# Attention, mLSTM and expert layers on one core: an order per engine, maxima in bfloat16, a mask from 32-row products

## What is computed

```
x = x + attention(layernorm(x), W_qkv, W_out)        # 16 heads of width 16, causal
x = x + mlstm(layernorm(x), ctx, ctx, gates)         # 8 heads of width 32
x = x + experts(layernorm(x), router, up, down)      # 8 experts, 2 for each token

attn = softmax(q k^T / 4 + mask);  out = attn v      # mask: -1e10 where key > query
out = out.reshape(B, -1, S);  y = einsum("bds,nhd->bsd", out, W_out)
log_d = lf[t] - lf[s] + i[s], causal;  m = max_s(log_d);  d = exp(log_d - m)
h = (q k^T / sqrt(32) * d) v / (max(|sum_s|, exp(-m)) + 5e-5), then RMS-normed per head
```

## Time and profile before

| what | us |
|---|---|
| median of 3 runs | 974.06 (972.89 to 978.18) |
| the profiled execution | 972.35 |
| its span, first to last instruction | 970.6 |
| TensorE busy in the span | 880.4 (91%) |
| VectorE, ScalarE, GpSimd busy | 616.0, 490.8, 501.4 |
| mean clock granted to TensorE | 0.965 of full |

### The profile page before, as it was taken

One profiled execution on the slowest core, in us unless ns is written; L12 is line 12 of the kernel. 1 busy time (PEld: TensorE's weight loads), 2 busy tenths in 40 slices (PEclk: granted clock), 3 DMA queues, 4 the chain that ended last, 5 costly groups with the idle time before them and its releaser, 6 DMA issues.

```text
span 970.6 us, 31715 instructions
## 1 busy us (share of the span) xinstructions
PE 880.4 (91%) x11877; PEld 652.7 (67%) x11966; DVE 616.0 (63%) x1324; ACT 490.8 (51%) x839; POOL 501.4 (52%) x705
## 2 busy tenths in 40 slices
PE   4899999989997688999998998999999999999995
PEld 3566666766765445556665776878787878778783
DVE  4766776676767455679898677555555555555552
ACT  3566767767765556556664643333333333333331
POOL 2454756665665433357777677633444434444432
PEclk9899999999998988889998999999999999999998
DMA  8213343334244654355564433433232333233222
GB/s 273 66 24 88 84 112 113 80 89 140 78 88 138 131 174 146 101 160 177 186 193 134 122 73 91 99 67 51 47 51 46 53 49 51 46 51 51 46 35 23
DMA packets 133198, 92.97 MB, mean 96 GB/s; under 512 B 75712, under 2 KB 114112, under 8 KB 132928
## 3 DMA queue, kind: packets, MB, share of 16 engines
q1 hardware_dynamic: 119760, 73.10, 27.2%
q0 software_dynamic: 13296, 17.83, 11.2%
HBM read 54.65 MB, written 37.32 MB: 95 GB/s over the span
## 4 chain that ended last, share of the span: by engine, by line
PE 63%; DVE 11%; ACT 7%; DMA 6%; issue 4%; POOL 3%; SPq 3%; POOLq 0%; DVEq 0%; ACTq 0%
PE pair L963 19%; PE pair L977 10%; PE pair L979 7%; PE pair L665 4%; PE pair L687 3%; PE pair L701 3%; DMA o_scr<-On 3%; DMA STG<-wup_in 2%; PE pair L840 2%; PE pair L638 2%; ACT PT L1360 2%; PE pair L714 2%; PE pair L854 2%; DVE SD L1159 2%; PE pair L929 1%
## 5 line engine op out<-in xcount | busy, mean ns | idle before, releaser
L963 PE MATMUL pair<-XTs,WU 128*128 128x128 bf16 x3408 | 284.0, 219 | 7.7 <-DVE XTs L1303 4.0
L963 PEld LDWEIGHTS pair<-XTs,WU 128*128 x3408 | 237.7, 98 | 75.4 <-issue 12.2
L1637 POOL DMA_INDIRECT out_d<-XB x71 | 115.6, 1629 | 202.5 <-DVE XB L1325 168.8
L1503 ACT ACTIVATE Hf<-pair 128x512 f32<-128x512 f32 x142 | 84.9, 598 | 217.2 <-PE pair L963 217.0
L977 PE MATMUL pair<-WD,Hh 128*128 x479 | 181.1, 379 | 0.2
L1316 DVE CAST Hh<-Hf 128x512 bf16<-128x512 f32 x142 | 64.3, 453 | 164.5 <-ACT Hf L1503 160.2
L979 PE MATMUL pair<-WD,Hl 128*128 x568 | 154.8, 272 | 4.8
L1548 POOL TENSOR_SCALAR_AFFINE_SELECT PT<-PT 128x512 f32<-128x512 f32 (+1 forms) x96 | 74.7, 793 | 56.8 <-ACT PT L1354 52.0
L1318 DVE TENSOR_TENSOR Hl<-Hf,Hh 128x512 bf16<-128x512 f32 x142 | 99.7, 702 | 4.9
L1049 DVE TENSOR_REDUCE mxn<-pair 128x4 f32<-128x1024 f32 x64 | 75.2, 1216 | 27.4 <-PE pair L646 27.3
L1610 POOL DMA_INDIRECT xs_scr<-XB,WGf x64 | 68.6, 1071 | 28.2 <-issue 16.7
(11 more groups left out here) (245 smaller groups left out, 1756.5 us busy)
## 6 DMA issues: line engine op xcount, KB each, us to landing
XB<-xs_scr SPq DMA_DIRECT2D x71, 130.0 KB, 2.1
STG<-wup_in SPq DMA_DIRECT2D x32, 256.0 KB, 4.7
q_scr<-SPL SPq DMA_DIRECT2D x16, 512.0 KB, 4.2
STG<-wdn_in SPq DMA_DIRECT2D x32, 256.0 KB, 3.0
o_scr<-On SPq DMA_DIRECT2D x32, 128.0 KB, 4.1
Mm<-o_scr SPq DMA_DIRECT2D x16, 256.0 KB, 2.9
CnT<-ctxt_in SPq DMA_DIRECT2D x16, 256.0 KB, 4.5
CX<-ctx_in SPq DMA_DIRECT2D x16, 256.0 KB, 3.9
```

The source lines that it names most:

```text
L963: t = e.matmul(upb(j, k)[:, 128 * (fm % 4):128 * (fm % 4) + 128], WU[:, bass.ds(reg[j] * 4096 + off, 128)], XTs[:, r, hx, dk, :], start=n ...
L1503: e.activation(Hf[:, r, hs], upb(j, k), ACT.Gelu).then_inc(gel.sem, 1)
L1637: e.indirect_dma_start(out=out, out_offset=bass.IndirectOffsetOnAxis(ap=XS[:, i % NX, 256:257].bitcast(I32), axis=0), in_=Yf[:, i % NY, :] ...
```

## The change

**An order for each engine.** attn_steps takes an engine and reads a table ROUND, written like ORDER. On TensorE the cyclic order of a round stays, but for MG, which moves ahead of AX. ScalarE does the context split (A6c) and A6n earlier in the round. On GpSimd A6s stands ahead of the first weight split, the second split and A0s stand at the end of the round, A6c ahead of T2. The first gate chain (GT, Gs, Gp) is moved earlier on TensorE and ScalarE; on VectorE the step Gs now follows AX of the last item. The lines of ORDER are new as well.

```diff
+ROUND = {
+    "tensor": "T0:1:1 GT:15 S0:0 VX:0 T2:1 A4:2 MG:0 weights:0:2 AX:0 S1:-1:0 T0:0:0 PV:1 S1:-1:1 QK:-2",
...
+def attn_steps(engine):
+    parts = 0
+    for i in range(-4, B + 3):
+        for kind, lag, u in words(ROUND[engine]):
+            b = i - lag
...
-    "gpsimd": "sc:0 B4p:2 sc:0 R6:5 sc:0 split:0 split:0 B5s:2 rest:0:0 rest:0:1 rest:0:2 split:0",
+    "gpsimd": "R6:5 rest:0:0 sc:0 split:0 sc:0 split:0 split:0 B5s:2 B4p:1 sc:0 rest:0:1 rest:0:2",
...
+                    w.wait_ge(l_lm, 16)
                     for u in range(2):
                         pair_free(w, kind, *key, u)
                         for jj in range(2):
-                            e.matmul(out_[u][:, jj, :].rearrange("p (g c) -> p g c", c=wd)[:, :, wd - 128:wd], idb[:, :],
-                                     mkb[:, :].rearrange("p (a c) -> p a c", a=1).broadcast_to([128, n, 128]),
+                            rows = slice(64 * u + 32 * jj, 64 * u + 32 * jj + 32)
+                            e.matmul(out_[u][:, jj, :].rearrange("p (g c) -> p g c", c=wd)[:, :, wd - 128:wd], LM[rows, 0, :],
+                                     LM[rows, 1, :].rearrange("p (a c) -> p a c", a=1).broadcast_to([32, n, 128]),
                                      start=True, stop=False, skip_group_check=True)
...
                     else:
                         pair_left(w, 1)
+                        w.wait_ge(b_init, 1)
...
-            e.tensor_scalar(mv[:, :, 2], mv[:, :, 1], 1e-5, None, ALU.add).then_inc(var.sem, 1)
+            e.tensor_tensor(mv[:, :, 2], mv[:, :, 1], CF[:, C_EP:C_EP + 1].broadcast_to([128, 2]), ALU.add).then_inc(var.sem, 1)
...
                 elif kind == "S1":
+                    w.wait_ge(mpT.sem, mpT.at(b - 1))
+                    w.wait_ge(p_init.sem, p_init.at("Mp0"))
                     for u in range(2):
                         w.wait_ge(s1m.sem, s1m.at(b, P, u))
-                        e.tensor_reduce(mxn[:, 1, P, 2 * u:2 * u + 2, :], pair_of("S1", b, P, u)[:, :, :].rearrange("p j (r c) -> p j r c", r=2),
+                        e.tensor_reduce(Mph[:, 1, P, 2 * u:2 * u + 2, :], pair_of("S1", b, P, u)[:, :, :].rearrange("p j (r c) -> p j r c", r=2),
                                         AX.X, ALU.max, negate=True).then_inc(mx1.sem, 1)
...
-                elif kind == "Mp":
-                    w.wait_ge(mx1.sem, mx1.at(b, 1, 1))
-                    w.wait_ge(mx0.sem, mx0.at(b, 1))
-                    w.wait_ge(mpT.sem, mpT.at(b - 1))
-                    w.wait_ge(p_init.sem, p_init.at("Mp0"))
-                    e.tensor_copy(Mph[:, :, :, 0], mxv).then_inc(dvc.sem, dvc.up())
-                    w.wait_ge(dvc.sem, dvc.n)
-                    e.tensor_tensor(Mph[:, :, :, 1], mxv, Mph[:, :, :, 0], ALU.subtract).then_inc(mp_.sem, 1)
...
+            w.wait_ge(s0m.sem, s0m.at(B - 1, 1))
+            e.tensor_copy(mkb, CF[:, C_MASK:C_MASK + 128])
             link(e.memset(dsel[:, :, :], 0.0))
...
-                    e.tensor_scalar(XB[:, t0:t0 + 4, 259], KM, -1.0, 8.0, ALU.mult, ALU.add)
+                    e.tensor_tensor(XB[:, t0:t0 + 4, 259], CF[:, C_EK:C_EK + 1].broadcast_to([128, 4]), KM, ALU.subtract)
```

More of the change, by code:

```diff
@@ new lines, with words @@
+ROUND = {
[5 rows of a table added]
+}
+LIMITS = {"S1": (0, B - 1), "T0": (0, B - 1), "PV": (0, B - 2), "A0s": (0, B - 1), "A0n": (0, B - 1), "QK": (0, B - 1), "A6s": (0, B - 4),
+          "A6n": (0, B - 4), "S0": (0, B - 1), "VX": (0, B), "T2": (0, B - 1), "A6c": (0, B - 4), "A4": (0, B - 2), "AX": (-2, B), "MG": (0, B)}
+def words(line):
+    for word in line.split():
+        kind, lag, *u = word.split(":")
+        yield kind, int(lag), int(u[0]) if u else 0
+def attn_steps(engine):
[3 more added lines that the diff above has]
+            b = i - lag
+            if kind == "load":
+                if ok(b):
+                    yield kind, 2 * b, 0
+                    yield kind, 2 * b + 1, 0
+            elif kind == "split":
+                if ok(b):
+                    yield kind, parts, 0
+                    parts += 1
+            elif kind not in LIMITS:
+                if b == 0:
+                    yield kind, u, 0
+            elif LIMITS[kind][0] <= b <= LIMITS[kind][1]:
+                yield kind, b, u
@@ L169 @@
 ORDER = {
[5 rows of a table removed]
-}
-def entries(engine):
-    for word in ORDER[engine].split():
-        kind, lag, *u = word.split(":")
-        yield kind, int(lag), int(u[0]) if u else 0
[5 rows of a table added]
+}
 def mlstm_steps(engine):
@@ L190, in mlstm_steps @@
     for i in range(B):
-        for kind, lag, u in entries(engine):
+        for kind, lag, u in words(ORDER[engine]):
             b = i - lag
@@ L243, in of, with build @@
     return [s[1:] for s in steps if s[0] == kind]
-def build(nc, x, ctx_in, ctx_t, wqkv, wout, wg, bg, gain, wr, br, wup, wdn, cst, out):
+def build(nc, x, ctx_in, ctx_t, wqkv, wout, wg, bg, gain, wr, br, wup, wdn, cst, msk, out):
     xs = nc.dram_tensor("xs_scr", (XROWS, ROW), F32, kind="Internal").ap()
@@ L333, in build @@
         wtmp = OTs[:, 2, :]
[L334 to L335 removed]
+        Mph = Mp[:, :, :, :, 0:2]
         ca.close()
@@ L376, in build @@
         Hf = sb("Hf", [128, 2, 1024], F32)
-        steps = list(attn_steps())
+        pe_attn, dve_attn, act_attn, pool_attn, sp_attn = (list(attn_steps(n)) for n in ROUND)
         pe_steps, dve_steps, act_steps, pool_steps, sp_steps = (list(mlstm_steps(n)) for n in ORDER)
         dvc, poc = Chain(sem("dve_chain")), Chain(sem("pool_chain"))
+        l_lm = sem("l_lm")
         l_c, l_w, l_wo, l_wg, l_z = sem("l_c"), (sem("l_w0"), sem("l_w1")), sem("l_wo"), sem("l_wg"), sem("l_z")
@@ L403, in chunk @@
             return src[:, 512 * k:512 * k + 512], v[:, :, 0, :], v[:, :, 1, :], STG[:, c % 2, :].rearrange("p (a w) -> p a w", w=width)
-        lns = [s[:2] for s in steps + dve_steps if s[0] in ("A0s", "A6s", "B5s")]
+        lns = [s[:2] for s in dve_attn + dve_steps if s[0] in ("A0s", "A6s", "B5s")]
         LNK = {k: i % 4 for i, k in enumerate(lns)}
@@ L433, in build @@
         users = []
-        for kind, b, P in steps:
+        for kind, b, P in pe_attn:
             if kind in ("S1", "T0"):
@@ L1036, in vector_attn @@
         def vector_attn(e, w):
-            for kind, b, P in steps:
+            for kind, b, P in dve_attn:
                 if kind == "weights":
@@ L1338, in scalar_attn @@
         def scalar_attn(e, w):
-            for kind, b, P in steps:
+            for kind, b, P in act_attn:
                 if kind == "weights" and b < 2:
@@ L1549, in causal @@
                                 channel_multiplier=-1).then_inc(done.sem, 1)
-            for kind, b, P in steps:
+            for kind, b, P in pool_attn:
                 if kind == "weights" and b == 2:
@@ L1688, in sync_attn @@
                             onesb[:, :].rearrange("p (a c) -> p a c", a=1).broadcast_to([128, 2, 128])).then_inc(l_on, 16)
-            for kind, b, P in steps:
+            for kind, b, P in sp_attn:
                 if kind == "load":
```

119 lines of the change are left out of this document (39 added, 80 removed), and 12 rows, old and new, of tables (ORDER, ROUND).

## The result

The changed kernel takes **960.0 us** (median of four runs, 954.6 to 962.8) beside 973.5 of the kernel before in the same comparison: a ratio of 0.985, with an interval of 0.982 to 0.988. In a second comparison with more runs it was 0.981 (0.978 to 0.984). It is faster, inside the range, and by 13.5 us where 26.1 were forecast.

A forecast was written before the change was run, and what follows sets the result against it. TensorE's time was taken as the bound, plus where it stands still or is clocked down. 13.0 + 1.1 + 3.5 + 8.5 = 26.1 us off the profiled 972.35 gave 946.3, or a median of 948.0, range 941 to 955.

The forecast's parts named there:

- S1's masks: Attention round on TensorE: 32-row mask products run side by side, gaining 0.4 us a round for S1 part 1.
- rival 2: Attention masks don't run side by side, or writes of four banks hold each other up: 958 us, chance 0.06.
- Rival 3: Attention round is set by the DMAs, not TensorE, so 13 us are lost: 961 us, chance 0.07.
- S0's masks: Attention round on TensorE: shorter masks for S0, whose second half still waits for ScalarE's evacuation, gain 0.3 us a round.
- The tail: Attention round, from T2's end to T0's start: 4.60 us becomes 4.33, a gain of 0.27 us a round.
- The first item: Start of the attention, where no tail runs beside the masks: three masks give 0.4 + 0.4 + 0.3 = 1.1 us.
- The end of the attention: Last full round: A6s ahead of the weight split and gates ahead of T2 shorten ScalarE's path, gaining 3.5 us.
- The mLSTM: New order removes TensorE's waits of B6 (3.0) and B5 (2.1) and clock falls (3.4): together 8.5 us.
- Rival 1: New waits of TensorE for busy VectorE eat the mLSTM's gain: 956.5 us, chance 0.16.
- Rival 4: The mLSTM's slow half-clock stretch in the fourth item goes as well: 939.5 us, chance 0.11.
- tensor_tensor for tensor_scalar: VectorE's small operations in the mLSTM, slow beside GpSimd's products: the new form gains nothing.
- Rival 6: Shorter masks make TensorE stand still more and its clock fall to half once a round: 984 us, chance 0.06.

The follow-up runs named there:

- q_vector: Changed kernel with the queries evacuated from QK's PSUM pair by VectorE instead of ScalarE: 952.6 us, 0.977 of the kernel before.
- old_s0_mask: Changed kernel with the 128-row masks of before for S0 alone, S1 keeping the 32-row ones: 955.9 us, 0.982 of the kernel before.
- old_mlstm_again: Changed kernel with the mLSTM's steps in the old order on every engine, repeated on an undisturbed chip: 964.2 us, 0.992 of the kernel before.
- old_attention_again: Changed kernel with the attention's steps in the old order on every engine, masks still new, repeated on another chip: 970.1 us, 0.998 of the kernel before.
- the second group: Follow-up runs of several kernels on one disturbed chip, where all stood still together several times; the kernel before took 992.8 us there.

## Why the prediction came out as it did

The sign, the range and most of the places were right; the size was twice what was measured. In the span the change brought 13.2 us (13.5 in the medians), as 1.3 + 5.9 + 1.0 + 6.1 - 1.1, where 1.1 + 13.0 + 3.5 + 8.5 stood in the sum.

- **S1's masks, 0.4 a round: right.** 0.43 measured, the whole of what a round gained, and rival 2 (masks one after the other) fell with it. Rival 3, the pace of the DMAs, fell with q_vector's rounds of 17.62.
- **S0's masks, 0.3 a round: the step failed.** I asked what releases S0's second half, and not what releases the step behind it. VX's pair belongs to T0, whose exponentials come after ScalarE's evacuation, 5.56 us behind QK with any mask (old_s0_mask). A start right behind its releaser has no wait in its row, and that hid this one.
- **The tail, 0.27 a round: mis-sized, it was 0.** From T2's end to T0 4.61 us pass, and 4.60 passed. Of the two parts, TensorE's steps ahead of `SPL` took 2.43 us instead of 2.27, and T0 started 0.26 behind VectorE's `xTl` instead of 0.14. A gain of a quarter of a microsecond was put together from four numbers with an error of 0.1 each. That the wait ahead of T0 would be 1.2 us and released by `xTl` was right (1.33).
- **Together 0.43 a round, not 1.0**: 5.6 us over 13 rounds for 13.0. The trace has 5.9, with one fall of the clock at 50 us (1.6 us) against it and two rounds of before that were 0.6 and 1.1 us longer than those around them. I had expected the clock at 1.00 until 290 us.
- **The first item, 1.1:** 1.3 in this trace; but that mark lies between 46.7 and 50.5 us over all traces, so it shows nothing.
- **The end of the attention, 3.5: right where it arises, wrong in what is left.** T0 of the last item came 4.2 us sooner relative to the rounds. Then PV waited 2.27 us for GpSimd's masks, which stand behind two fills and a weight split, and ran at half clock. I had followed ScalarE alone. At X1 1.0 is left. The added wait of D for `dsel` was there (1.90 us) and covered, as I said: X1 still waits 5.58 us for `Mm`.

```profile
321.45 0.38 PE L791 MATMUL pair<-idb,LM 128*128 128x256 bf16 x2 [1.90 <-issue]
...
334.96 1.09 PE L882 MATMUL pair<-CF,Mm 128*128 128x128 f32 x4 [5.58 <-DMA Mm<-o_scr]
```

- **The mLSTM, 8.5: nearly right in the sum, otherwise made.** 6.1 in this trace, 5.8 to 7.6 over most. Most of the waits of B6 and B5 went, and with B6's the two falls of the clock, 1.7 us each, that I had put to them. Rival 1 came true by 3 us, as S waiting for VectorE. Rival 4 came true too: the stretch of half clock went with the order, up to 7 us in these two traces. Its size is luck, since the same waits gave 3, 14 and 17 us of half clock, and the shorter stretch that the new order has instead lasts from 0 to 14. That the sum came near 8.5 is so in part luck as well. Then a part is lost again behind the two waits at the end, which I hadn't looked for since before has them too, shorter.
- **tensor_tensor for tensor_scalar, nothing: right.** With the old order and the new form R2's first operation is as slow as with the old form, 1.70 us in the mean of six where 1.71 was. With the new order it is 0.16. VectorE's group of old_mlstm_again and of after from 300 to 550 us:

```profile
L1183 DVE TENSOR_TENSOR XB<-CF,WGf 128x4 f32<-128x4 f32 x6 | 10.2, 1700 | 0.0
```

```profile
L1183 DVE TENSOR_TENSOR XB<-CF,WGf 128x4 f32<-128x4 f32 x6 | 0.9, 158 | 0.0
```

  What the form didn't do, its place did, though a part has only moved: the third operation of B4's chain (L1158), 0.17 us alone, now takes 1.08 beside such products, 3 us more in all. By the Trainium skill (GPSIMD Engine Reference, Key points) two SBUF inputs bring the contention just as a 2-port mode does; this trace agrees.
- **Rival 6, slower, 0.06:** not for this change, but for its masks without the new order. They give the round 0.43 us and, in the old order, the clock takes more than that back: 240.3 us for 13 rounds that took 237.0 before. (The bfloat16 maxima came with them; no run parts the two in the old order.) The order of the attention, which I had counted at a quarter of a microsecond a round and 3.5 us at the end, is worth 13 to 17 us of the time (old_attention_again).

The experts' 1.1 us stay unexplained; from the first expert product to the end of the span it is 422.0 us before and 423.1 after, and 421.3 to 423.8 over all traces outside the second group.

## What to carry over

For each step that gets shorter, look up what releases the next one, its PSUM buffer's last reader too, and compare the time of its start with the end of that release, since a row without a wait may be held up all the same. Where TensorE waits at one place in a loop, shortening its other work lengthens that wait and can cost its clock, as here where 1.04 us became 1.38: judge an edit by the granted clock over the loop as well as by the length of one round. A stretch of half clock in a single trace is one draw; look at several traces before its whole length goes into a sum. Gains ahead of a chain of DMAs should be priced at what arrives behind it.
